# Two-layer graph attention block: scores kept by parity, the cross terms swapped through memory, four loads issued by ScalarE

## What is computed

```python
def layer(h, params):
    wl, b_l, ws, b_s, wr, b_r, g, beta = params
    u = jnp.einsum('bid,bjd->bij', h, h) / temper
    a = jax.nn.softmax(u, axis=-1)
    delta = a * adjacency_matrix
    attn = delta / (jnp.sum(delta, axis=-1, keepdims=True) + 1e-10)
    hl = h @ wl.T + b_l
    hs = h @ ws.T + b_s
    hr = h @ wr.T + b_r
    diag_a = jnp.diagonal(attn, axis1=1, axis2=2)
    ctx = jnp.einsum('bij,bjd->bid', attn * upper, hl) + diag_a[..., None] * hs + jnp.einsum('bij,bjd->bid', attn * lower, hr)
    mean = ctx.mean(-1, keepdims=True)
    var = ctx.var(-1, keepdims=True)
    o = (ctx - mean) / jnp.sqrt(var + LN_EPS) * g + beta
    return (jax.nn.relu(o), None)
...
x = _layernorm(x + both_layers(x), axis=-1)
```

## Time and profile before

| | |
|---|---|
| median of 3 runs | 1632.81 us (1631.94 to 1633.05) |
| the profiled execution, its own time | 1631.82 us |
| its span | 1630.1 us |
| PE busy, share of the span | 1605.1 us, 98% |
| DVE busy | 1398.9 us, 86% |
| POOL busy | 1212.5 us, 74% |
| ACT busy | 1078.0 us, 66% |
| granted TensorE clock | 0.997 of full |

### The profile page before, as it was taken

One profiled execution on the slowest core, in us unless ns is written; L12 is line 12 of the kernel. 1 busy time (PEld: TensorE's weight loads), 2 busy tenths in 40 slices (PEclk: granted clock), 3 DMA queues, 4 the chain that ended last, 5 costly groups with the idle time before them and its releaser, 6 DMA issues.

```text
span 1630.1 us, 35740 instructions
## 1 busy us (share of the span) xinstructions
PE 1605.1 (98%) x9509; PEld 1597.9 (98%) x9509; DVE 1398.9 (86%) x4368; ACT 1078.0 (66%) x2835; POOL 1212.5 (74%) x1542
## 2 busy tenths in 40 slices
PE   8999999999999999999999999999999999999996
PEld 7899999999999999999999999999999999999995
DVE  7788888888888888888888888888888888888886
ACT  6566666666666666666666666666666666666654
POOL 5677777777777777777777777777777777777764
PEclk9999999999999999999999999999999999999998
DMA  5444444444444444444444444444444444444431
GB/s 175 102 110 107 114 114 107 111 107 116 107 114 111 110 107 113 114 107 112 107 115 106 114 112 110 109 110 115 107 114 109 112 106 114 114 108 111 108 93 45
DMA packets 463943, 179.17 MB, mean 110 GB/s; under 512 B 348592, under 2 KB 462896, under 8 KB 463920
## 3 DMA queue, kind: packets, MB, share of 16 engines
q1 hardware_dynamic: 463920, 178.91, 43.3%
HBM read 112.92 MB, written 65.86 MB: 110 GB/s over the span
## 4 chain that ended last, share of the span: by engine, by line
PE 92%; DMA 1%; DVE 1%; SPq 1%; POOL 1%; ACT 1%; issue 1%; DVEq 0%; POOLq 0%; ACTq 0%
PE p_proj L430 70%; PE p_gather L517 16%; PE p_score L424 5%; PE p_score L446 1%; DMA rows_mem<-rows_blocks 1%; SPq L366 1%; DMA attnT_whole<-attn_mem 1%; SPq L351 0%; POOL rstd L1173 0%; POOL attnT L1163 0%; DVE stats L623 0%; POOL attnT_split L1169 0%; DVE p_gather L646 0%; DVE p_gather L619 0%; DVE rows_blocks L725 0%
## 5 line engine op out<-in xcount | busy, mean ns | idle before, releaser
L430 PE MATMUL p_proj<-w,hT_layer 128*128 128x384 f32 x6912 | 1368.6, 339 | 0.9 <-DVE w L744 0.5
L430 PEld LDWEIGHTS p_proj<-w,hT_layer 128*128 128x128 f32 x6912 | 1162.5, 188 | 2.0 <-POOL w L1220 1.0
L281 POOL TENSOR_TENSOR proj_split<-proj,proj_split 128x768 fp32r<-128x768 f32 x253 | 467.6, 1848 | 182.3 <-ACT proj_split L943 181.9
L517 PE MATMUL p_gather<-proj_split,attnT_split 128*128 128x384 f32 x1536 | 309.3, 335 | 2.3 <-POOL attnT_split L1169 1.6
L1173 POOL TENSOR_TENSOR rstd<-veps,neg_half 128x1 f32<-128x1 f32 x384 | 206.8, 549 | 91.9 <-DVE veps L632 82.6
L517 PEld LDWEIGHTS p_gather<-proj_split,attnT_split 128*128 128x128 f32 x1536 | 269.9, 188 | 4.7 <-POOL attnT_split L1169 2.7
L943 ACT ACTIVATE proj_split<-proj 128x768 fp32r<-128x768 f32 x256 | 214.9, 839 | 84.7 <-DVE proj L688 83.7
L688 DVE TENSOR_TENSOR proj<-p_proj,bias_all 128x768 f32<-128x768 f32 x256 | 244.9, 957 | 12.9 <-PE p_proj L430 5.1
L1169 POOL TENSOR_TENSOR attnT_split<-attnT,attnT_split 128x256 fp32r<-128x256 f32 x256 | 190.3, 743 | 71.0 <-ACT attnT_split L934 70.9
L947 ACT ACTIVATE o<-y,nbias,rstd 128x384 f32<-128x384 f32 x128 | 90.7, 709 | 227.0 <-POOL nbias L1177 227.0
L424 PE MATMUL p_score<-hT_layer 128*128 128x256 f32 x768 | 216.6, 283 | 1.8 <-DVE rows L720 0.8
(11 more groups left out here) (59 smaller groups left out, 1598.3 us busy)
## 6 DMA issues: line engine op xcount, KB each, us to landing
xt_raw<-xT SPq DMA_DIRECT2D x128, 192.0 KB, 2.6
xn<-x SPq DMA_DIRECT2D x128, 192.0 KB, 2.4
out<-o SPq DMA_DIRECT2D x128, 192.0 KB, 2.0
rows_mem<-rows_blocks SPq DMA_DIRECT2D x124, 192.0 KB, 1.9
rowsT<-rows_mem SPq DMA_DIRECT2D x496, 48.0 KB, 2.4
adj_layer<-adj SPq DMA_DIRECT2D x256, 64.0 KB, 1.9
attn_mem<-attn_blocks SPq DMA_DIRECT2D x124, 128.0 KB, 1.7
attnT_whole<-attn_mem SPq DMA_DIRECT2D x496, 32.0 KB, 2.2
```

The lines of the kernel that those rows point to most:

```text
L281: op.tensor_tensor(proj_split[u][:, LO], proj[u][:, UP:LOW + 1, :], proj_split[u][:, HI].bitcast(F32), ALU.subtract).then_inc(s_proj_lo[k], 1)
L430: return nc.tensor.matmul(p_proj[:, which, 0:D], hT_of(k, b)[:, slot, st, c, :], w[:, k, which, mv, c, :], start=(n == 0), stop=(n == 8))
L517: last = nc.tensor.matmul(home(k, b)[:, 0:D], AT_split[u][:, st, side, :], proj_split[u][:, mv, side, :], start=(side == UP and n == 0), s ...
```

## The change

Four things are changed.

- The two PSUM banks are now one for even and one for odd iterations. Each holds the parts of both layers (2 x 2 x 128 columns), so the bank is full: E moves to an SBUF tile `exps`, and `diagonal` reads the identity from SBUF.
- In iterations 4 to 126 there is no cross matmul. ACT copies X of both layers in one instruction (`copy_cross`, 128x256), DVE transposes it in blocks (`turn_cross`, 128x256), SP stores it beside the blocks of the attention (`store_swap`, 4 x 128 columns instead of 2 x 128) and loads it swapped (`load_swap`), and POOL adds X and its transpose (`add_cross`). `scaled_scores` reads that sum, in the next iteration.
- The scores are therefore taken one graph earlier (graph i+2 of layer 1 and i-2 of layer 2 in iteration i, `pair_slice`), all six matmuls beside `project_self` of layer 1. The inputs are split one graph earlier too, and `hT[0]` has four slots.
- The four loads of the transposed rows (`load_rows`) are issued by ACT instead of SP, between `output_squares` and `high_projections(1, i - 3)`.

The new pieces:

```diff
+        def parts(k, slot):
+            return p_score[slot % 2][:, 2 * k:2 * k + 2, :]
...
+            def turn_cross(i, slot):
+                done(dve, s_crossed, i - 4)
+                if live(i, i + 2):
+                    nc.vector.transpose(blocks[:, slot, 2:4].rearrange("p k n -> p (k n)"),
+                                        crossed[:].rearrange("p k n -> p (k n)")).then_inc(s_cross_blocks, 1)
```

DVE's `iteration` of the steady part:

```diff
                 normalise_layer1(i - 1, q)
                 low_rows(i - 2, p)
+                if not isinstance(i, int) or i > 4:
+                    done(dve, s_cross_sum, i - 5)
+                    output_mean(i - 5)
+                    if live(i, i + 1):
+                        scaled_scores(0, i + 1, q, cross_sum[:, 0])
+                    scaled_scores(1, i - 3, q, cross_sum[:, 1])
+                add_bias(0, i, True)
+                block_rows(i - 1)
                 mask(i, 1, i - 3, q)
                 if live(i, i + 1):
-                    done(dve, s_score[0], i + 1)
+                    mask(i, 0, i + 1, q)
                 diagonal(1, i - 3, q)
                 if live(i, i + 1):
-                    scaled_scores(0, i + 1, q)
-                add_bias(0, i, True)
-                block_rows(i - 1)
-                if live(i, i + 1):
-                    mask(i, 0, i + 1, q)
                     diagonal(0, i + 1, q)
+                turn_cross(i, p)
                 add_bias(0, i, False)
                 row_moments(1, i - 4, p)
...
                 add_bias(1, i - 3, True)
-                scaled_scores(1, i - 2, p)
-                output_mean(i - 4)
                 add_bias(1, i - 3, False)
```

ACT's:

```diff
                 relu_rows(i, i - 2, p)
-                if live(i, i + 1):
-                    cross_scores(0, i + 1)
                 high_rows(i - 2, p)
-                high_sides(1, i - 4)
-                normalise_rows(i, i - 1)
                 if live(i, i + 1):
                     exponentials(0, i + 1, q)
+                exponentials(1, i - 3, q)
+                normalise_rows(i, i - 1)
+                high_sides(1, i - 4)
+                high_projections(0, i)
+                copy_cross(i, p)
                 high_sides(0, i)
...
-                cross_scores(1, i - 2)
+                if not direct_rows(i, i - 1):
+                    load_rows(i - 1, q)
+                high_projections(1, i - 3)
                 if live(i, i - 5):
                     finish(i, q)
-                high_projections(1, i - 3)
-                exponentials(1, i - 2, p)
```

POOL's, at its start:

```diff
                 low_projections(nc.gpsimd, pool, 1, i - 4)
                 attn_arrived(i - 1, q)
+                if not isinstance(i, int) or i > 4:
+                    add_cross(0, 2)
+                deviation_layer1(i - 1)
                 cut_sides(1, i - 4)
-                deviation_layer1(i - 1)
                 low_sides(1, i - 4)
```

More of the change, by code:

```diff
@@ L183, in graph_block @@
         s_warm = sem("s_warm")
+        s_blank = sem("s_blank")
         def per_layer(name):
@@ L259, in attnT_count, with cross_count, swapped @@
             return b + 1 if k == 0 else b - G + 8
+        def cross_count(b):
+            return b + 1 if b < 6 else b - G + 6
         def rowsT_count(b):
             return b + 1 if b < 2 else b - G + 5
-        def attn_layers(i):
-            first = 0 if live(i, i + 1) and not direct(i, 0, i + 1) else 1
-            last = 2 if live(i, i - 3) and not direct(i, 1, i - 3) else 1
-            return first, last
+        def swapped(i):
+            return (1, 2) if isinstance(i, int) and i == G - 1 else (0, 4)
         def done_apart(eng, s, b):
@@ new lines, in store_swap @@
+            def store_swap(i, slot):
+                first, last = swapped(i)
+                if isinstance(i, int) and i == 3:
+                    sp.wait_ge(s_blank, 1)
+                    sp.wait_ge(s_attn_blocks[0], 1)
+                elif last == 4:
+                    sp.wait_ge(s_cross_blocks, i - 3)
+                else:
+                    sp.wait_ge(s_attn_blocks[1], i - 2)
+                sp.dma_start(swap_mem[slot][:, first:last], blocks[:, slot, first:last]).then_inc(
+                    s_swap_out[slot], 16)
@@ new lines, in load_swap @@
+            def load_swap(i, slot):
+                first, last = swapped(i)
+                sp.wait_ge(s_swap_out[slot], swap_moves(i, slot))
+                pieces = swap_mem[slot].rearrange("(r a) k (s b) -> s a k r b", a=B, b=B)
+                for s in range(4):
+                    rows_s = slice(s * B, (s + 1) * B)
+                    if last - first == 1:
+                        sp.dma_start(whole[rows_s, first, :].rearrange("a (r b) -> a r b", b=B),
+                                     pieces[s][:, first]).then_inc(s_swap_in[slot], 16)
+                    else:
+                        sp.dma_start(whole[rows_s, first:last, :].rearrange("a k (r b) -> a k r b", b=B),
+                                     pieces[s][:, first:last]).then_inc(s_swap_in[slot], 16)
@@ L464, in project_sides, with project_self @@
                     last.then_inc(s_proj[k], 1)
-            def project_self(k, b, slot, before, b_last, scored=None, first=0, last_part=8):
+            def project_self(k, b, slot, before, b_last, scored=None, first=0, last_part=8, pair=None):
                 done(pe, s_self_biased[before], b_last)
@@ L1081, in close @@
                     high_rows(G - 3, 1)
+                    exponentials(1, G - 4, 0)
                     normalise_rows(i, G - 2)
@@ L1162, in cut_sides @@
             def cut_sides(k, b):
-                nc.gpsimd.tensor_tensor(AT[k][:], AT_whole[:, k].unsqueeze(1).broadcast_to([P, 2, N]), sides[:],
+                nc.gpsimd.tensor_tensor(AT[k][:], whole[:, k].unsqueeze(1).broadcast_to([P, 2, N]), sides[:],
                                         ALU.mult).then_inc(s_side[k], 1)
@@ L1222, in low_weights, with add_cross @@
                                             ALU.subtract).then_inc(s_w_lo[k][which], 1)
+            def add_cross(first, last):
+                nc.gpsimd.tensor_tensor(cross_sum[:, first:last], crossed[:, first:last],
+                                        whole[:, 2 + first:2 + last], ALU.add).then_inc(s_cross_sum, 1)
             def attn_arrived(i, slot):
-                pool.wait_ge(s_attn_in[slot], attn_moves(i, slot) * 4)
+                pool.wait_ge(s_swap_in[slot], swap_moves(i, slot) * 4)
             pool.wait_ge(s_setup, 5)
```

298 lines of the change are left out of this document (171 added, 127 removed).

## The result

The changed kernel takes 1828.26 us as a median of 4 runs (1827.28 to 1829.56); the kernel before, on the same chip, 1632.38 us (1630.94 to 1633.05). The ratio is 1.120, with an interval of 1.118 to 1.122: 196 us are lost. The profiled execution took 1829.56 us, its span is 1827.8 us, and the granted clock is 0.996 in place of 0.997, so the clock has no part in it. One run of one experiment, the kernel with the four loads back on SP, took 4029.71 us where its other three took 1902.86 to 1904.11; it is left out of that experiment's ratio.

What follows compares the result with a forecast made beforehand. PE's issue rate was taken to bound the kernel at 12.44 us an iteration. After the change, 13.3 us for DVE and ACT plus 1.2 us of contention gave 14.5 us, 256 us lost over 122 iterations: 1889 us, range 1720 to 2010.

Steps and rivals of the forecast that it cites:

- a ring of DVE and ACT: Each iteration's DVE and ACT work waits on the other's; 0.36 us slack before, 13.3 us without contention after, replacing PE's bound.
- ACT's stretch: ACT's part from DVE's layer-2 bias to the next `low_rows`, with `finish` added: 4.12 us.
- DVE's stretch: DVE's part from `low_rows` to the layer-2 bias: 8.05 us before, 8.84 with `turn_cross`, layer-2 score and output mean.
- The new wait for `normalise_rows`: DVE's block transpose of the rows waits for ACT's normalisation, now behind both exponentials: about 0.35 us.
- Contention of two SBUF operands: Four DVE masks and diagonals an iteration wait behind POOL's SBUF instructions: 1.2 us, bounds 0 to 3.3; chance 0.48.
- The heavy rival: Masks and diagonals repeatedly meet POOL's long instruction: up to 3.3 us of waits, 16.6 us an iteration, 2140 us; chance 0.08.
- the one without contention: Masks and diagonals don't wait for POOL: 13.3 us an iteration, 1738 us, up to 1800; chance 0.34.
- POOL is a tie: From the layer-2 bias to DVE's scores, the ways over POOL's `add_cross` and over the relu both take 4.6 us; no cost.
- ACT's issues cost nothing: ACT's four row-load issues, 2.58 us, fit into its waits and the place `finish` leaves: no cost.
- The path through memory costs nothing: From `turn_cross` through store and swapped loads to `add_cross`: 6.3 us needed, 8 us available, no cost.
- The sum: 13.3 us plus 1.2 us gives 14.5 us an iteration against 12.44; 256 us over 122 iterations, 1889 us.
- What would show it: Profile signs: chain through DVE and ACT, L780 and L790 medians above 0.3 us, longer POOL instructions, PE busy some 85%.

Runs made afterwards that it cites:

- both causes taken away: Changed kernel with mask and diagonal operands in PSUM, layer-2 bias ahead of `output_rows`, and `high_input` behind ACT's four DMA issues: 1694.19 us, ratio 1.039.

## Why the prediction was right, and where it was not

- **PE isn't the bound, a ring of DVE and ACT is.** Right. PE waits for POOL's low sides and for DVE's bias, at the two places named; its share is 90%, not 85%.
- **ACT's stretch, 4.12 us.** 4.11 us.
- **DVE's stretch, 8.84 us without waits.** 8.25 us. This term was too large, by 0.6 us. 0.16 of it is because start to start is shorter than a duration where instructions follow one another: the mean costs 0.06 us (from 502.30 to 502.36) and not its duration of 0.15, `turn_cross` 0.37 and not 0.44. There I had read durations of a row where the next row's start was what mattered. The larger part, 0.40, is that steps which changed neighbours were shorter in their new place, and these I had taken from start to start, in the old order: score to bias 0.22 for 0.36, a block transpose to what follows 0.23 for 0.31, the layer-1 self bias to what follows 0.44 for 0.62.
- **The new wait for `normalise_rows`, 0.35 us.** 0.46 us. That wait was real and paid: the experiment that removes it gained 82 us, though more than half of that was contention that changed with the phase.
- **Contention of two SBUF operands, 1.2 us, bounds 0 to 3.3.** 1.19 us in the iteration shown. The mechanism was shown twice apart from all else: taken out of the changed kernel (medians of 521 and 380 ns fall to 254 and 266) and put alone into the kernel before. That the number agrees so well is in good part luck, since its working took POOL's work as coming at any moment. It doesn't: the ring and POOL's list have a fixed phase, in every iteration the same three of four meet. I had read 0.8 of a POOL instruction as the time held. The runs show that DVE is held to the POOL instruction's end, and that the missing part is what DVE came late, and what it has left to do then: the last diagonal starts 0.07 us behind POOL's 0.75, is held for the other 0.68 and needs 0.14 more, 0.82 in place of 0.25.
- **The heavy rival, 3.3 us, and the one without contention** fall: the first because the masks met the short POOL instructions only, and the fourth instruction none; the second with the 601 and 536 ns of L780 and L790.
- **POOL is a tie.** Right for the segment that I counted: `finish` off the ring gave 9 us and not 70. But I had looked at that segment alone. The rest of POOL's list is a second ring (high sides, low sides, `rstd`, `output_rows`); its wait of 0.32 us, together with some 0.3 us that the experiment's own order cost, is why taking away the contention gave 0.7 us and not 1.19 an iteration.
- **ACT's issues cost nothing.** Right here: 2.61 us inside a wait of 4.53. It needs the late bias; with the bias early they and their landing were on the chain.
- **The path through memory costs nothing.** Right here, with the same limit: with the early bias POOL waited 0.5 us an iteration for it, and near 12.7 us it was the end of the chain, where its 7.5 us exceed what the shorter period leaves.
- **The sum.** 14.5 us an iteration were predicted and 14.01 measured. The DVE term is the whole of the difference (-0.6, and +0.1 for the wait), so 1889 became 1828 us. That the fill would cost nothing was wrong by some 5 us.
- **What would show it.** That the chain would run over DVE and ACT was wrong: the profile's page has 52% of it on POOL. The ring was to be seen in the timelines and the waits. POOL's instructions did get longer, but by little: the cut from 741 to 762 ns, `low_projections` from 1849 to 1870. The bill is DVE's. L744 was also not the only DVE work with two SBUF operands before: three low projections at the start and the end (L281, 953 ns) were such.

## What to carry to other kernels

Before an edit is costed in a pipeline that one engine bounds by a hair, find the ring of waits behind that engine and its slack: here 0.36 us of slack decided a change whose gain was 0.12 us, and after the first ring came a second over POOL, a third over ACT's queue and a fourth through memory, and the loss was gone only when all had been shortened. What was added to a ring is counted from start to start, and a step that moves can change its length with its neighbours. And an operand moved from PSUM to SBUF changes the timing of every DVE instruction that POOL's wide SBUF work can meet; how much it costs depends on where the two lists stand against each other, so it has to be read from the timeline, not from an average.

## What the runs showed of the hardware

- A mask or diagonal on DVE with two SBUF operands that meets a running cut, low side or low projection of POOL ends some 0.15 us after it (0.13 to 0.16 in all of the 42 long cases between 400 and 600 us of the changed kernel). In the kernel before with its operands moved it is so in 23 of 27 cases over 0.32 us, and 0.29 us in the other four, which came in the last 0.05 us of a cut.
- A running POOL instruction on one column (`rstd`, 0.55 us) doesn't hold it: in the kernel before with its operands moved, the four masks between 400 and 600 us that came 0.21 to 0.27 us into one took 0.28 us.
- The price lies on DVE in these kernels, where its instruction is the short one; POOL's own grew by 0.02 us. Where three DVE and three POOL instructions of 384 columns ran against each other, both paid: POOL's took 1.32 to 1.33 us where the two others of the same line (L1220) took 1.01 to 1.02.
- One operand in PSUM was enough to avoid it: the 246 diagonals of the steady part took at most 289 ns beside the same POOL list.
- Issuing the four row loads takes ACT's queue 2.61 us (2.76 with both causes taken away), as it took SP's (2.58): an issue costs 0.65 us on either. The landing is less sure than the issue, 2.4 us for the rows before and 2.7 after, as medians, and 3.33 us where it was on the chain.
